# A two-layer graph network on one core: node and end stage in groups of two blocks instead of four, with the first relative rows and two gather slots placed beside the node stage's tiles

## The reference

```python
# layer 0
mean_edge = segment_sum(edge_attr, dst) / max(count, 1)
out = concat([x, mean_edge, global_feats[0] for every node])
x = layernorm(x + softplus(out @ W.T) - log(2))
# layer 1
h = relu(_ln(x @ W1 + b1, g1, bt1))
edge_weights = sigmoid(relu(concat([h[src], h[dst]]) @ We1 + be1) @ We2 + be2)
aggr = segment_sum(edge_weights * h[src], dst)
gate = sigmoid(concat([h, aggr]) @ Wg + bg)
h_new = gate * aggr + (1 - gate) * h
x = layernorm(x + _ln(h_new, g2, bt2))
```

## Time and profile before

| what | us |
|---|---|
| median of three runs | 2201.44 |
| lowest and highest | 2198.95, 2205.48 |
| the profiled execution, its own time | 2202.91 |
| its span in the profile | 2201.2 |
| busy PE / DVE / ACT / POOL | 1621.5 / 1705.9 / 1070.7 / 1437.0 |
| mean granted TensorE clock | 0.761 of full speed |

### The profile page before, as it was taken

How to read it: one execution, slowest core, us unless ns; L and a number is a source line. 1 busy time by engine, 2 the same in 40 slices (tenths; PEclk the granted TensorE clock), 3 DMA queues, 4 the chain that set the end, 5 groups by cost and what they waited for, 6 DMA issues and landing times.

```text
span 2201.2 us, 43991 instructions
## 1 busy us (share of the span) xinstructions
PE 1621.5 (74%) x13238; PEld 1452.1 (66%) x13239; DVE 1705.9 (77%) x7202; ACT 1070.7 (49%) x2826; POOL 1437.0 (65%) x1437
## 2 busy tenths in 40 slices
PE   4999996898477467777877877767667767877780
PEld 3777775776366467777777876766666667777640
DVE  7777886595899578887888887888876776777666
ACT  0111111375776046665666665766654544555325
POOL 4354430152777777777777777777777777777765
PEclk9999998687555557766767677898788786767675
DMA  7788898014544546556556566666666566666402
GB/s 275 261 298 286 289 336 286 27 47 157 176 127 138 159 127 177 169 170 181 172 166 181 158 181 189 179 189 181 176 198 195 173 193 192 188 188 186 131 1 59
DMA packets 279081, 394.16 MB, mean 179 GB/s; under 512 B 75155, under 2 KB 178612, under 8 KB 278715
## 3 DMA queue, kind: packets, MB, share of 16 engines
q1 hardware_dynamic: 217155, 226.47, 32.4%
q0 software_dynamic: 57408, 156.84, 24.5%
q10 hardware_dynamic: 4280, 8.03, 1.1%
HBM read 376.07 MB, written 15.12 MB: 178 GB/s over the span
## 4 chain that ended last, share of the span: by engine, by line
POOL 46%; PE 24%; issue 19%; DVE 7%; DMA 2%; DVEq 1%; ACTq 1%; ACT 1%; SPq 0%; POOLq 0%
POOL x_rows L894 34%; POOL ring L894 11%; PE bank L495 9%; PE bank L502 3%; PE bank L1289 3%; PE bank L542 2%; DVE bank L531 1%; PE bank L1261 1%; DMA x_rows<-src_table,lane_src 1%; DVE sums L1813 1%; PE bank L1233 1%; DMA ring<-src_table,lane_src 1%; DVE stats L1722 1%; PE bank L1298 1%; ACTq L974 1%
## 5 line engine op out<-in xcount | busy, mean ns | idle before, releaser
L894 POOL DMA_INDIRECT x_rows<-src_table,lane_src x900 | 888.9, 988 | 298.9 <-issue 271.8
L531 DVE SCALAR_TENSOR_TENSOR bank<-bank,we_all 128x128 f32<-128x128 f32 x1686 | 431.6, 324 | 11.1
L894 POOL DMA_INDIRECT ring<-src_table,lane_src x296 | 286.0, 966 | 90.2 <-issue 89.3
L546 DVE TENSOR_TENSOR sums<-sums,bank 128x128 f32 (+1 forms) x814 | 206.2, 253 | 150.1 <-issue 89.3
L1369 PE MATMUL bank<-ring,sums 128*128 128x128 f32 x980 | 274.1, 369 | 46.6 <-DVE bank L531 46.1
L527 DVE TENSOR_TENSOR bank<-bank,x_rows 128x512 f32<-128x512 f32 x225 | 146.4, 696 | 194.5 <-DMA x_rows<-src_table,lane_src 194.4
L1100 ACT ACTIVATE ring<-sums,be_all 128x4 f32<-128x4 f32 (+1 forms) x124 | 36.9, 297 | 508.8 <-DVE bank L531 508.8
L542 PEld LDWEIGHTS bank<-weighted,x_rows 128*128 128x128 f32 x1800 | 280.2, 245 | 0.0
L542 PE MATMUL bank<-weighted,x_rows 128*128 128x40 f32 x1800 | 279.0, 325 | 0.0
L522 PE MATMUL bank<-ring,onehot_t 120*128 120x128 bf16 x1196 | 135.7, 282 | 161.8 <-issue 84.6
L495 PE MATMUL bank<-ring 128*64 128x128 f32 x3128 | 221.8, 285 | 30.4 <-issue 25.3
(11 more groups left out here) (250 smaller groups left out, 3386.2 us busy)
## 6 DMA issues: line engine op xcount, KB each, us to landing
ring<-in_edge_attr SPq DMA_DIRECT2D x195, 512.0 KB, 5.0
ring<-rel_table SPq DMA_DIRECT2D x74, 512.0 KB
ring<-cell_table SPq DMA_DIRECT2D x121, 256.0 KB
ring<-src_table SPq DMA_DIRECT2D x144, 128.0 KB
x_rows<-src_table,lane_src POOLq DMA_INDIRECT x900
ring<-dst_table SPq DMA_DIRECT2D x299, 32.0 KB
ring<-src_table SPq DMA_DIRECT2D x104, 64.0 KB
src_table<-ring SPq DMA_DIRECT2D x12, 512.0 KB, 3.7
```

The source lines that it names most:

```text
L531: last = eng.scalar_tensor_tensor(hid[:, j, :], hid[:, j, :], 0.0, wide["we2"][:, :], ALU.max, ALU.mult, accum_out=out[:, j:j + 1])
L546: return eng.tensor_tensor(table[..., bass.ds(start, width)], table[..., bass.ds(start, width)], part, ALU.add)
L894: eng.indirect_dma_start(gathered(c)[:, j, :], None, src_table, bass.IndirectOffsetOnAxis(ap=lane_src[:, t:t + 1], axis=0)).then_inc(gathe ...
```

## The change

GB becomes 2, so there are 25 groups in the edge stage's xw, the node stage, x1_offset and the end stage. GROUP_EVERY becomes 7, since 25 groups have to fit into 196 pairs. The temporary tiles of the node stage take half the room of before; behind them (node_end) lie the two gather slots and the three slots of relative rows. The window of dst rows moves to the start of ring. SP loads the first relative rows at the start of the node stage, as soon as the edge stage has been done, and POOL no longer waits for part2 at chunk 6. The three small tiles of the end stage that lay in the first slot of `rest` now lie across both its slots.

```diff
-    GB = 4
+    GB = 2
...
+        rest_at = at[0]
         rest = temp(GC)
-        assert n_blocks <= P
-        moments_all = rest[:, 0, 0:2 * n_blocks].rearrange("p (b t) -> p b t", t=2)
-        rstd_all = rest[:, 0, 2 * P:2 * P + n_blocks]
-        offset_all = rest[:, 0, 3 * P:3 * P + n_blocks]
+        assert n_blocks <= P and 3 * P + n_blocks <= 2 * GC
+        moments_all = ring[:, rest_at:rest_at + 2 * n_blocks].rearrange("p (b t) -> p b t", t=2)
+        rstd_all = ring[:, rest_at + 2 * P:rest_at + 2 * P + n_blocks]
+        offset_all = ring[:, rest_at + 3 * P:rest_at + 3 * P + n_blocks]
...
-        dst_at = at[0]
         dst_out = temp(GC * PARTS // 2, BF16)
-
-
+        node_end = at[0]
...
-        ring_slots = list(range(R_SLOTS * SLOT, 12 * GC, SLOT)) + list(range(12 * GC, dst_at, SLOT))
+        rel_at = node_end + (G_SLOTS - own_slots) * SLOT
         gather_slots = [x_rows_flat[:, i * SLOT:(i + 1) * SLOT] for i in range(own_slots)] + \
-            [ring[:, a:a + SLOT] for a in ring_slots] + [counts[:, a:a + SLOT] for a in range(0, padded - SLOT + 1, SLOT)]
-        assert len(gather_slots) >= G_SLOTS
-
-        rel = ring[:, 0:R_SLOTS * SLOT].bitcast(BF16).rearrange("w (s c e) -> w s c e", s=R_SLOTS, c=R_BATCH)
+            [ring[:, a:a + SLOT] for a in range(node_end, rel_at, SLOT)]
+        assert len(gather_slots) == G_SLOTS and rel_at + R_SLOTS * SLOT <= 21 * BANK
+
+        rel = ring[:, rel_at:rel_at + R_SLOTS * SLOT].bitcast(BF16).rearrange("w (s c e) -> w s c e", s=R_SLOTS, c=R_BATCH)
...
-        window = ring[0:WIN_ROWS, dst_at:dst_at + Q_SLOTS * P // 2].bitcast(BF16).rearrange("w (q f) -> w q f", q=Q_SLOTS)
+        window = ring[0:WIN_ROWS, 0:Q_SLOTS * P // 2].bitcast(BF16).rearrange("w (q f) -> w q f", q=Q_SLOTS)
...
-        spare = ring_slots[G_SLOTS - own_slots]
+        spare = Q_SLOTS * P // 2
...
-        GROUP_EVERY = 8
+        GROUP_EVERY = 7
...
-                if g == n_groups - 1:
-
-                    loaded(eng, "rel_table", row_groups)
-                    need(eng, "norm1", g)
-                    need(eng, "norm1_act", g)
-                    for k in range(R_SLOTS):
-                        rel_load(k)
...
+            eng.wait_ge(done("acc_all"), 1)
+            loaded(eng, "rel_table", row_groups)
+            for k in range(R_SLOTS):
+                rel_load(k)
             run_stages(n_groups, [(0, src_table_out), (DST_AT - NORM2_AT - 2, dst_table_out)])
...
-                if c == own_slots:
-                    eng.wait_ge(done("part2"), n_groups)
```

2 lines of the change are left out of this document (1 added, 1 removed).

## The result

| | before | after |
|---|---|---|
| device time, median | 2201.77 us (2198.95 to 2205.48) | 2227.68 us (2221.29 to 2234.19, 4 runs) |
| ratio | | 1.0114, 95% interval 1.0085 to 1.0143 |
| profiled execution, span | 2202.9, 2201.2 | 2234.2, 2232.5 |
| mean granted TensorE clock in it | 0.761 | 0.752 |
| first gather starts | 548.93 | 576.93 |

The change costs 25 us by the ratio (26 by the two medians), where 17.5 were forecast. The profiled execution is the longest of the four after, 6.5 us above the median, so what is read from it is somewhat more than the median run's.

A forecast was written before the change was run, and what follows sets the result against it. POOL's gathers were taken to bound the long middle, leaving the first gather's start and the end stage to count. Node stage +7, first wait -1.5, mixing +4 and output +8 made +17.5 us: 2219 us, range 2203 to 2242.

The forecast's parts named there:

- Edge stage: Stage before the node stage: spreading the x-by-w_node products moves work, not time; 0, with ends of -6 and +5 us.
- rival 3: It evens out: half of the node stage's loss and 6 us gained in the edge stage; +5 us, 2206; 11%.
- Fill and rounds 5 to 8: Node stage start: five rounds of 2.8 us, 14.0; then four at PE's lower clock of 4.6 us, 18.4.
- Rounds 9 to 11: Node stage, first full rounds, bound by VectorE: 4.5 us each with handing over, 13.5 us together.
- Full rounds 12 to 25: Node stage with rest and part2 joined: VectorE bounds at 5.2 us a round, PE's 4 us beside it; 72.8 us.
- Rival 2: PE's clock falls in the node stage: its 4 us become 6.4, +17 over 14 rounds, 4 in the drain; 2240; 14%.
- VectorE's cost per group: Node stage full rounds: VectorE's halved work, per-group costs, norm1, rest and part2 make 5.2 us a round.
- Drain: Node stage end, rounds 26 to 33: dst_out slots wait for table writes, 4.1 us a round; 31.8 us.
- Early relative rows: Loads moved to the node stage's start shorten POOL's 2.16 us wait before the first weighted sum; -1.5 us.
- Gather stage, no change: POOL's gathers set the long middle and nothing in the change touches their pace; about 1541 us.
- Mixing +4 and output +8: End stage: POOL's mixing 1.70 us a group, +4 us; VectorE and ACT's output loop 2.19 us a group, +8 us.

The follow-up runs named there:

- laterel: The changed kernel with the first relative rows loaded late, behind the last source table write, as before; 2227.05 us, 1.0102 of the kernel before.
- node2: The changed kernel with its end stage in groups of four, but half of the last normalization left out; 2217.46 us, 1.0064 of the kernel before.
- node2b: The changed kernel with its end stage in groups of four, all four blocks normalised; 2221.04 us, 1.0094 of the kernel before.
- fill_after: The changed kernel with eight more bf16 matmuls of 128 columns in each node stage round; 2215.66 us, 1.0044 of the kernel before.
- count1: The changed kernel with the counts turned by one bf16 product instead of f32; 2211.72 us, 1.0049 of the kernel before.
- count1_fill: The changed kernel with counts turned by one bf16 product and eight added bf16 products a round; 2456.74 us, 1.0017 of the kernel before (2453.25).
- dve1: The changed kernel with DVE_BLOCKS 1 instead of 2, one norm1 block of a group given to ScalarE; 2221.17 us, 1.0083 of the kernel before.
- count1_before: The kernel before (groups of four) with the counts turned by one bf16 product; 2447.33 us, 0.998 of the kernel before (2453.25).

## Why the prediction came out as it did

The size was 9 us short (2219 against 2227.7) and inside the range of 2203 to 2242, and slower was given 0.81. The direction and its main reason, that a round does not shrink to 21/33, were right; the bound of the full rounds was not. By its own steps, measured in the profiled execution:

- **Edge stage, 0.** In this profile right: 309.4 us of TensorE in the stretch, and its end 0.7 us earlier. In the other eight profiles of groups of two it ends 4 to 8 us before that of the kernel before, around the -6 given as an end and the 6 us of rival 3.
- **Fill and rounds 5 to 8, 14.0 and 18.4 us.** 15.8 and 17.8 us.
- **Rounds 9 to 11, 13.5 us.** 15.5, over which the clock came up (0.50 at 435 us, 1.00 from 445).
- **Full rounds 12 to 25, 72.8 us.** 90.2. This is the step that failed: "PE's work for two blocks at the full clock is some 4 us ... and lies beside that". The work is 4.3 of 5 us at the upper level, and the level fell at about 460 us. What the forecast leaned on, that PE fully busy had been followed by a rising clock before the change (0.57 from 430 to 440 us with PE busy 10.00 of 10, then 1.00), is not a rule: here PE was busy 10.00 of 10 us in stretch after stretch from 470 to 520 at the lower level. Rival 2 had the mechanism and priced the full rounds at +17; they came out at +17.4 in the profile, the agreement in part by luck: its slow round of 6.4 us was 6.97, but only ten or so of the fourteen were slow. Its 4 us in the drain were 1.5. It had 14%, and that was too little. The Trainium skill, TensorE: Matmul & The Clock Gate, section What's actually happening, says that the clock follows how busy the engine has been; on these rows busy time in the profile does not foretell it, and the measurement decides.
- **VectorE's cost per group, 5.2 us a round.** Right where the clock is up: 5.27 in each of the seven profiles of the changed kernel, laterel, node2, node2b, fill_after, count1 and count1_fill.
- **Drain, 31.8 us.** 33.3, by other parts: 4.5 to 6.3 us in its first rounds (part0 on ACT at 542.85, 548.29, 552.80 and 559.07), at the lower level, and 3.3 to 3.4 in the rest, as a write of dst_table lands in 2.0 us and not 2.7.
- **Early relative rows, -1.5.** Nothing that shows.
- **Gather stage, no change.** Right: 1539.3 us against 1539.9. The earlier trace rows shows POOL's longest wait for PE; over the stage there are ten, 4.9 us in all, and not one.
- **Mixing +4 and output +8.** 4 together. Two terms were mis-sized: 0.25 us of hand-over a group, added to POOL's two operations, was 0.05 (1.55 us of period for 0.73 and 0.78 of work), and output on two blocks takes 0.64 us, not 0.82. Over 24 groups that is 24 x 0.15 = 3.6 us in mixing and 24 x 0.19 = 4.6 in output, the 8 us.
- **Rival 3, 2206.** Its sum is off: half of the node stage's loss and 6 us off 17.5 leave +8, not +5.

The total is close in part by luck. Up to the first gather 5.5 us were forecast and some 21 measured at the median (node2b), 15 too little; at the end 12 were forecast and 4 measured, 8 too much. Inside the first of these, the node stage's own loss, 23 to 29 us, is hidden in part by the shorter edge stage.

Open: what lets the clock fall or rise. In the profile after, the last gap of TensorE before it fell was 0.60 us, at 459.06. But in node2b the level stayed up from 440 to 480 us with TensorE busy 8.4 to 8.7 of 10 us, so such gaps alone don't bring it down.

## What to carry to other kernels

Price an engine's share of a round at both levels of TensorE's clock, and if it is over the bound at the lower one, treat the round as able to take either length; that a stretch before the change stayed up is no promise. Small products are worth a look: taking the f32 off a one-column product gave 14 us in groups of two, about what the added products gave there (15), and 5 us in groups of four, where the added products cost 5; its slow round was also shorter, 6.41 us against 6.97. Smaller groups halve what is work and keep what is per instruction and per hand-over, and with a pipeline of twelve rounds that was a loss even where the clock was up: 156 us from the edge stage to the first gather (dve1, count1_fill) against 148. Compare whole stages in more than one profile: the one pair of before and after hid some 7 us of the edge stage.

## What was not expected of the hardware

- TensorE fully busy at the lower level of its clock for 50 us on end, and six runs of one kernel spread over 24 us (dve1, 2206.28 to 2230.43). The kernel before spread over 19 us in 17 runs on that chip (2197.74 to 2216.95).
- The product that turns a row of counts is one output column, yet as f32 four records of it take 0.95 us at the lower level and 0.55 at the upper, against 1.23 and 0.71 for four records of the mean product with its 128 columns.
- One of the three chips ran the kernel before at 2453 us instead of 2203. It was not profiled there, but count1_before was, and in it all of the difference is in the gather stage: it starts its first gather at 543.43 and its last at 2332.34 us, 1789 us against 1540. A wait appears in POOL's group there that the kernel before doesn't have on its own chip (idle before it, by what ended it):

```profile
L894 POOL DMA_INDIRECT x_rows<-src_table,lane_src x900 | 899.9, 1000 | 474.1 <-issue 242.2 <-remote 175.5 <-PE bank L542 35.0
L894 POOL DMA_INDIRECT ring<-src_table,lane_src x296 | 296.0, 1000 | 141.2 <-issue 79.8 <-remote 61.4
```

  237 us of waits that the profile puts down to "remote". An instruction itself takes 1000 ns, against 988. The full rounds of the node stage are as long as on the other chips (7.5 to 7.8 us here, 5.27 in count1_fill), so the difference is in how fast the gathers land or are taken up, which no run here tells apart.
